# Splitting the rows of the tile two ahead after the first chunk of gelus, not ahead of the fourth, in an expert loop on one core

## What is computed

```
scores = sigmoid(xf @ gate_w + bias)                # 8 experts, the top 2 of a token are used
up = einsum('th,ehi->tei', xf, up_w) + up_b         # 256 -> 1024
hact = gelu(up)
eo = einsum('tei,eih->teh', hact, down_w) + down_b  # 1024 -> 256
combined = einsum('teh,te->th', eo * 0.1, w)
shared = (gelu(xf @ sw_up + sb_up) @ sw_down + sb_down) * 0.1
out = (shared + combined); out = out / (max(abs(out), axis=-1) + 1e-6)
x = x + gb * out
```

## Time and profile before

| what | us |
|---|---|
| median of three runs | 877.2 |
| lowest and highest | 875.07, 881.87 |
| the profiled execution, its own time | 877.31 |
| its span in the trace | 875.4 |
| PE busy, share of the span | 828.9, 95% |
| DVE busy | 611.5, 70% |
| ACT busy | 455.1, 52% |
| POOL busy | 458.6, 52% |

### The profile page before, as it was taken

How to read it: one execution, slowest core, us unless ns; L and a number is a source line. 1 busy time by engine, 2 the same in 40 slices (tenths; PEclk the granted TensorE clock), 3 DMA queues, 4 the chain that set the end, 5 groups by cost and what they waited for, 6 DMA issues and landing times.

```text
span 875.4 us, 21221 instructions
## 1 busy us (share of the span) xinstructions
PE 828.9 (95%) x5973; PEld 776.9 (89%) x5974; DVE 611.5 (70%) x1566; ACT 455.1 (52%) x859; POOL 458.6 (52%) x521
## 2 busy tenths in 40 slices
PE   6999999899999999999799999989999999999982
PEld 5778887889889989987799999979999999999982
DVE  5788988668777777767847566666666666666653
ACT  3865654244443544445476555565566555556630
POOL 4554320224765765675204656646656665665565
PEclk9999999899999999999999999989999999999996
DMA  8220000381242243232652333434433343444442
GB/s 300 75 97 1 1 0 1 89 253 25 101 125 38 88 123 77 67 103 91 227 198 76 89 88 98 147 96 94 94 86 86 87 93 93 92 92 86 86 89 52
DMA packets 68491, 83.25 MB, mean 95 GB/s; under 512 B 22976, under 2 KB 56730, under 8 KB 68288
## 3 DMA queue, kind: packets, MB, share of 16 engines
q0 software_dynamic: 25792, 39.92, 19.6%
q1 hardware_dynamic: 41808, 41.64, 15.1%
q10 hardware_dynamic: 816, 0.79, 0.3%
HBM read 45.43 MB, written 41.55 MB: 99 GB/s over the span
## 4 chain that ended last, share of the span: by engine, by line
PE 28%; issue 7%; DVE 4%; DMA 3%; ACT 3%; POOL 2%; DVEq 2%; ACTq 1%; POOLq 0%
PE psUp L1971 14%; PE psY L1996 13%; DMA gx<-shared_part,meta 2%; ACT gu L2034 1%; DVEq L995 1%; DMA shared_part<-ys,widx 1%; POOL out L2243 1%; PE psH L1943 1%; DVE gTl L2099 1%; ACT gTh L2039 1%; DVE yc L2120 1%; DVE top L2138 1%; POOL shared_part L2233 1%; DVE fin L2147 0%; ACTq L995 0%
## 5 line engine op out<-in xcount | busy, mean ns | idle before, releaser
L1971 PE MATMUL psUp<-eT,wup 128*128 128x256 f32 x1632 | 206.3, 287 | 5.5 <-DVE eT L2094 4.2
L1971 PEld LDWEIGHTS psUp<-eT,wup 128*128 128x128 f32 x1632 | 202.2, 195 | 6.5 <-issue 6.3
L1996 PE MATMUL psY<-wdn,gTh 128*128 128x256 f32 x1088 | 200.5, 286 | 0.0
L1996 PEld LDWEIGHTS psY<-wdn,gTh 128*128 128x128 f32 x1088 | 169.4, 192 | 0.0
L1996 PE MATMUL psY<-wdn,gTl 128*128 128x256 f32 x544 | 154.3, 284 | 0.0
L2243 POOL DMA_INDIRECT out<-fin,oidx x68 | 109.3, 1608 | 23.2 <-issue 15.9
L2034 ACT ACTIVATE gu<-psUp,ubias 128x256 f32<-128x256 f32 x272 | 113.4, 468 | 8.0 <-DVE gTl L2099 4.1
L2053 ACT ACTIVATE ys<-yc,meta 128x256 f32<-128x256 f32 x68 | 31.0, 503 | 162.6 <-DVE yc L2120 162.6
L2233 POOL DMA_INDIRECT shared_part<-ys,widx x68 | 71.4, 1050 | 79.5 <-issue 49.6
L2099 DVE TENSOR_TENSOR gTl<-gu,gTh 128x512 fp32r<-128x512 f32 x136 | 93.7, 689 | 27.4 <-ACT gTh L2039 24.7
L2224 POOL DMA_INDIRECT gx<-shared_part,meta x68 | 68.0, 1001 | 84.0 <-DMA shared_part<-ys,widx 62.3
(11 more groups left out here) (325 smaller groups left out, 1392.2 us busy)
## 6 DMA issues: line engine op xcount, KB each, us to landing
hin<-expert_in SPq DMA_DIRECT2D x36, 256.0 KB
X<-in_L_attn_x SPq DMA_DIRECT2D x8, 512.0 KB, 7.8
X<-bo_row POOLq DMA_DIRECT2D x8, 512.0 KB, 5.6
shared_part<-prow SPq DMA_DIRECT2D x8, 512.0 KB, 6.0
shared_part<-sh SPq DMA_DIRECT2D x8, 512.0 KB
out<-X SPq DMA_DIRECT2D x8, 512.0 KB, 4.3
raw_up<-in_L_ffn_up_w SPq DMA_DIRECT2D x3, 1024.0 KB, 5.6
raw_dn<-in_L_ffn_down_w SPq DMA_DIRECT2D x3, 1024.0 KB, 9.7
```

The lines of the kernel that those rows point to most:

```text
L1971: mm = nc.tensor.matmul(psU[:, c, (m % 2) * TR:(m % 2 + 1) * TR], wup[s][:, a, k, m * P:(m + 1) * P], eT[:, u, b, k], start=(n == 0), stop ...
L1996: mm = nc.tensor.matmul(psE[:, u, h * C:(h + 1) * C], (gTh, gTl)[a][:, u, m, h * P:(h + 1) * P], wdn[s][:, b, m], start=(n == 0), stop=(n ...
```

## The change

`high(j + 2)` moves from ahead of chunk 3 to ahead of chunk 1 in ACT's order. `low(j + 2)` moves from behind the third `low_g` to right behind the first in DVE's order, ahead of `largest`. No operation is added or taken away. The start-up ahead of the loop passes its own `turn` and is as it was. PE's, GpSimd's and SyncE's orders are the same.

```diff
-            def chunks(j, u, e, turn=MC - 1):
+            def chunks(j, u, e, turn=1):
 
                 for c in range(MC):
                     if c == turn:
...
                 if more:
                     low_g(j + 1, 1 - u, 0)
+                    low(j + 2, u)
                 if later(j, 1):
                     largest(j - 1)
...
                         end(j, u, True)
-                        low(j + 2, u)
                         low_g(j + 1, 1 - u, MC - 1)
...
                     end(j, u, more)
                     if more:
-                        low(j + 2, u)
                         low_g(j + 1, 1 - u, MC - 1)
```

## The result

The changed kernel is slower: 883.25 us in the median of 19 runs (879.69 to 886.73) against 876.84 us of before in 19 runs (874.82 to 881.87). The ratio is 1.0065 with a 95% interval of 1.0049 to 1.0081, which is 4.3 to 7.1 us; 883.8 us was forecast. The profiled execution took 882.95 us with a span of 881.1.

A forecast was written before the change was run, and what follows sets the result against it. The prediction took a loop of DVE and ACT beside PE, not PE, to set the end. From the profiled time, 877.3 + 7.7 (b) - 1.2 (c) + 0 (part one) = 883.8 us; 8-in-10 range 876 to 888.

The forecast's parts named there:

- What bounds the kernel: Expert loop: a second loop on DVE and ACT, 11.76 us a body, runs beside PE's 11.84 without waiting for PE.
- Part one: PE ahead of `up`: avoided waits and slow matmuls gain PE 6.35 us, of which 0 reaches the end.
- 2.80 us of slow matmuls: PE's `up` at 582.09: 48 matmuls took 8.66 us, not 5.86; counted as avoided with the 2.75 us gap.
- wait of the transposes for the rows: PE at 572.99: the 1.55 us ahead of the transposes wait for a transfer and stay.
- Part two (b): Fourth chunk's gelus on ACT wait for the second `low_g`, delayed by `low`: 0.27 us a body, 7.7 us in all.
- two bodies taken at 0.60 us: The bodies near 500 us and with the weight split behind 570 us: the whole 0.60 us counts in each.
- Part two (a): ACT at `high` waits 0.65 us once for PE's transposes; costs nothing as long as the lag is above this floor.
- floor under the lag: As rival: ACT's wait at `high` holds the loop 3.0 us behind PE, adding 2.7 to 2.9: 880.1 us, chance 0.13.
- Part two (c): End of the loop: late bodies no longer wait for PE's `psY`, taking 1.2 us off.
- bounds of the terms: (b) 1.8 to 8.9 us, (c) 1.0 to 1.5, part one 0 to -6.35; together given as 876 to 886.
- marks named ahead: Changed profile: DVE's bodies 12.0 us apart, gelu waits in each body, small PE gaps, no `psY` wait, tail as long.
- PE's two gaps: PE's waits ahead of `up` behind `low`, 0.80 us at 469.58 and 2.75 at 582.09, were to vanish.

The follow-up runs named there:

- gu4_after: The changed kernel with four gelu buffers instead of two: 875.98 us, ratio 0.9987 to the kernel before.
- mid: The changed kernel with `high` ahead of the third chunk on ACT and `low` behind the second `low_g` on DVE: 879.52 us, ratio 1.0013 to the kernel before.
- its control: The kernel before with four gelu buffers instead of two: 877.46 us, ratio 0.9992 to the kernel before.
- before_again: The kernel before, unedited, run once more for a second profile: 874.11 us, one run.
- act_only: The kernel before with only `high` moved ahead of the second chunk on ACT, `low` where it was: 880.37 us, ratio 1.0048 to the kernel before.
- dve_only: The kernel before with only `low` moved behind the first `low_g` on DVE, `high` still ahead of the fourth chunk: 967.81 us, ratio 1.1021 to the kernel before.
- second pair: Second profiles of the unedited kernel before and the unedited changed kernel: 874.11 and 881.66 us, one run each.
- after_again: The changed kernel, with no further edit, run once more for a second profile: 881.66 us, one run.
- low_second: The changed kernel with `low` behind the second `low_g` on DVE instead of the first: 880.51 us, ratio 1.0031 to the kernel before.
- gu4_low_second: The changed kernel with four gelu buffers and `low` behind the second `low_g` on DVE: 881.20 us, ratio 1.0018 to the kernel before.

## Why the prediction was right

**What bounds the kernel.** Right: the loop of DVE and ACT beside PE is what counts. Three kernels in which PE's long gap ahead of `up` is gone or down to 0.43 us (the change, `gu4_after`, `mid`) show no time clearly under before.

**Part one, PE's 6.35 us.** Given back before the end, as forecast: taken as 0, and shown by `gu4_after` against its control and by `mid`. The bound itself was read from one execution. The 2.80 us of slow matmuls don't belong to the gap as firmly as was counted: `before_again` lost 1.61 behind its gap of 2.65 us (7.47 - 5.86), and `act_only` 0.1 behind one of 2.75. One more detail was wrong: the wait of the transposes for the rows did not stay at 1.55 us but was 2.52 and 3.12 in the two profiles of the change. In the first of these the chain that ended last doesn't pass it. In the second it does (`hin`, 8.53 us from 566.96), so what it cost there is not settled.

**Part two (b), the buffer's wait.** The mechanism is settled by `gu4_after` with its control and by `dve_only`. The size: 0.23 us a body, not 0.27 (24 bodies of the second pair lost 5.61). The operation inserted took 0.60 us and the release 0.20, as put in; but the reduction and its followers took 1.27 us to the second `low_g` in both kinds of bodies (657.63 - 656.36), where before it was 1.36 in every second one. And of the two bodies taken at 0.60 us, the one with the weight split lost 0.15 in the second pair (18.95 to 19.10) and nothing in the first (18.84 to 18.72), the one at 500 us 0.54 in the second pair, with a wait for the transposes in it. The term was 7.7 us; the hardware loop lost 6.3 in the second pair and 3.2 in the first. Nothing was counted in the written-out bodies, and that was wrong for body 2: its fourth chunk's gelus wait for the second `low_g` in both profiles of the change (0.25 and 0.15 us in brackets), and it took 11.26 and 11.19 us where it had taken 10.91 and 10.90.

**Part two (a), the floor under the lag.** The rule as it was put holds ("costs nothing as long as the lag is above it"), but the sum has no term for the bodies in which the lag is below it, and there ACT's wait is in the loop that sets the end and counts in full. In `after_again` ACT waited there for 0.34 us in body 0, 0.69 in body 3 and 0.26 in body 4. Body 0 lost 0.46, and bodies 1 to 3 lost 1.12, of which 0.29 are body 2's wait for the buffer and 0.83 are body 3's. Timeline of ACT:

```profile
489.15 0.59 ACT L2027 CAST eT<-psH 128x512 fp32r<-128x512 f32 x1 [0.69 <-PE psH L1943]
...
501.10 0.59 ACT L2027 CAST eT<-psH 128x512 fp32r<-128x512 f32 x1 [0.26 <-PE psH L1943]
```

In the first profile of the change ACT had no such wait at all, so this term differs from one execution to the next. From the weight split on, the buffer's wait keeps the loop some 6.9 to 7.5 us behind PE, and the floor isn't met again. As a rival on its own it was given 880.1; `act_only` came to a ratio of 1.0048, which on 876.84 is 881.0.

**Part two (c), what there was to spare.** 1.2 us were taken off; bodies 30 to 32 gave 0.90, and the stretch behind them another 0.72, part of it again a wait for PE that is gone: the step from the last `yc` but one to the last is 8.52 us before and 8.12 after. In the first pair it was 0.91 and 1.36. What ended the rest of it was not looked into.

So 7.7 - 1.2 = 6.5 us was forecast. The second pair has 0.46 + 1.12 + 6.30 - 0.90 - 0.72 = 6.26, with (b) too large in the hardware loop, (a) and body 2 missing, and (c) too small, which nearly cancel. The first pair has only 1.49. The medians of 19 runs differ by 6.4. That the forecast met the median within 0.6 us is therefore in part luck: the mechanism and the 0.23 us a body are shown, the smaller terms are not known to better than some us. One slip in the forecast's own sums changes nothing here: its bounds of the terms add up to 871 to 885 us (877.3 + 1.8 - 1.5 - 6.35 and 877.3 + 8.9 - 1.0), not to "876 to 886".

Of the marks named ahead, the distances, PE's two gaps and the missing wait for `psY` came as said. Three did not. Idle time "in each body" ahead of the fourth chunk's gelus is there by the arithmetic of the rows, but bracketed in 4 of the 26 bodies of the hardware loop. PE's gaps ahead of `up` hardly show: PE is busy for 99.67 us of 100 from 600 to 700 and for 100.00 from 700 to 800, where 0.2 us a body had been forecast. That PE is held back can be seen from what it gets done: 836 matmuls in the 100 us from 600 on, where it was 847, the same 1.3% as between 11.84 and 11.99 us. For the same reason the chain that ended last is a poor guide here: PE has 16% of the span in it in the first profile of the change and 39% in the second, with the same steps of the bodies in both. And the tail was not "as long as before" but 0.7 to 1.4 us shorter.

## What to carry to other kernels

When the busiest engine's period and that of a second loop differ by 0.7% (11.84 and 11.76 us here), ask of a moved operation first what it does to the second loop: moving one ahead of others in an engine's queue makes each of them later by about its own length (0.5 to 0.6 us here), and whichever of them frees a buffer passes on what the waiting engine hadn't to spare (0.23 us here). To see such a loss, measure the distance from one body to the next on each engine; the list of waits hides it in overlaps. And a relief on the engine that looks full was worth nothing here while another chain set when the work ends.

## What the runs showed that was not expected

The place at which the expert loop begins moves by up to 5.4 us from one execution to another (the last `low_g` of the start-up at 446.34 to 451.72), with identical code ahead of it. A pair of single profiles would have put 4.2 of 5.7 us on the wrong stage. And what is left, taken from there on, is no measure of the whole either: it was 1.49 us in one pair and 6.26 in the other.

How long PE waits ahead of an `up` doesn't tell here whether the granted clock falls behind it. Timeline of PE in the kernel before (second profile) and then in `act_only`, with the window behind the gap in each:

```profile
580.47 7.47 PE L1971 MATMUL psUp<-eT,wup 128*128 128x256 f32 x48 [2.65 <-DVE eT L2094]
```

```profile
581.00:587.00 6.00, 6.00 (x40) 6.00 (x39) 4.08 (x8) 2.28 (x3) 2.25 (x2) 0.72 0.02 0
```

```profile
582.39 5.96 PE L1971 MATMUL psUp<-eT,wup 128*128 128x256 f32 x48 [2.75 <-DVE eT L2094]
```

```profile
583.00:589.00 6.00, 6.00 (x54) 6.00 (x53) 4.01 (x7) 2.29 (x3) 2.17 (x2) 1.00 0.02 0
```

The same wait of 2.75 us left the clock at full in one execution and was followed by 0.57 in another; waits of 2.15 us were followed by 7.50 us for the 48 matmuls in `low_second` and by 5.96 in `gu4_low_second`. What decides it was not found out.
